# Keys of a head quad in chunks of 128, 128 and 52, with both parts of the last chunk in one operand

## What is computed

```python
Q = (query @ Wq.T).reshape(B, T_q, N_HEADS, D_HEAD)
K = (context @ Wk.T).reshape(B, T_c, N_HEADS, D_HEAD)
V = (context @ Wv.T).reshape(B, T_c, N_HEADS, D_HEAD)
scores = jnp.einsum('bqhd,bkhd->bhqk', Q, K) / scale
attn = jax.nn.softmax(scores, axis=-1)
out = jnp.einsum('bhqk,bkhd->bqhd', attn, V).reshape(B, T_q, D)
return out @ Wo.T
```

## Time and profile before

| | |
|---|---|
| median of 3 runs | 2478.12 us (2477.07 to 2478.74) |
| span of the profiled execution, first to last instruction | 2474.6 us |
| PE busy | 2404.0 us (97%), 11592 matmuls |
| DVE, ACT, POOL busy | 1171.6, 942.9, 467.3 us |

### The profile page before, as it was taken

The page is one execution under the profiler, slowest core; times in us unless marked ns, Lnnn a source line. Parts: engine busy times, 40 slices in busy tenths (PEclk is TensorE's granted clock), DMA queues, the critical chain, the costliest instruction groups (busy, mean ns, idle before and its releaser), DMA issues.

```text
span 2474.6 us, 33004 instructions
## 1 busy us (share of the span) xinstructions
PE 2404.0 (97%) x11592; PEld 1975.2 (80%) x11592; DVE 1171.6 (47%) x1978; ACT 942.9 (38%) x1505; POOL 467.3 (19%) x554
## 2 busy tenths in 40 slices
PE   8998799999999999999999999999999999999999
PEld 4877578888888887788888888888888888888887
DVE  4999688888888887532212222212212212212211
ACT  3997444445444453443233223222222323323221
POOL 3777222222222222111001001001101101101100
PEclk9999989999999999999999999999999999999999
DMA  9454701211112111400000000000000000000000
GB/s 340 174 180 161 236 1 47 66 34 68 44 34 68 39 52 68 162 1 35 34 0 34 34 17 17 34 25 9 34 34 0 34 34 0 34 34 0 34 17 17
DMA packets 83115, 141.23 MB, mean 57 GB/s; under 512 B 18022, under 2 KB 18534, under 8 KB 82662
## 3 DMA queue, kind: packets, MB, share of 16 engines
q1 hardware_dynamic: 83072, 140.68, 16.4%
HBM read 79.42 MB, written 61.24 MB: 57 GB/s over the span
## 4 chain that ended last, share of the span: by engine, by line
PE 88%; DVE 5%; DMA 3%; issue 2%; ACT 1%; DVEq 1%; SPq 0%; POOL 0%; ACTq 0%
PE ps L359 76%; PE ps L1496 5%; PE ps L1476 2%; DMA xa<-in_x 1%; DMA x_scratch<-xa 1%; PE ps L1390 1%; DVE xa L1090 1%; DVE st L986 1%; PE ps L1329 1%; PE ps L1409 1%; PE ps L1354 1%; PE ps L1308 0%; DVE ql L1015 0%; DVE xt L1015 0%; DVE es L1192 0%
## 5 line engine op out<-in xcount | busy, mean ns | idle before, releaser
L1015 DVE TENSOR_TENSOR gtl<-ps,gth 128x512 fp32r<-128x512 f32 x256 | 177.1, 692 | 1088.9 <-ACT gth L904 1088.9
L359 PE MATMUL ps<-xt,wuh 128*128 (+1 forms) x2048 | 638.2, 393 | 5.0 <-DVE xt L1015 4.9
L902 ACT ACTIVATE ps<-ps,up_b 128x512 f32<-128x512 f32 x256 | 169.5, 662 | 990.2 <-PE ps L359 990.2
L359 PEld LDWEIGHTS ps<-xt,wuh 128*128 128x128 f32 x2048 | 383.6, 188 | 93.4 <-DVE xt L1015 8.9
L359 PE MATMUL ps<-wdl,gth 128*128 128x512 f32 x1024 | 402.3, 393 | 0.0
L359 PE MATMUL ps<-wdh,gtl 128*128 128x512 f32 x1024 | 402.1, 393 | 0.0
L359 PE MATMUL ps<-wdh,gth 128*128 128x512 f32 x1024 | 402.0, 393 | 0.0
L359 PE MATMUL ps<-xt,wul 128*128 (+1 forms) x1024 | 400.6, 391 | 0.0
L607 POOL TENSOR_TENSOR rstd<-var_e,mhalf 128x4 f32<-128x4 f32 x48 | 53.2, 1109 | 1306.6 <-DVE var_e L1004 1306.6
L668 POOL TENSOR_TENSOR es<-es,rinv 128x308 f32<-128x308 f32 x256 | 171.0, 700 | 447.0 <-DVE rinv L1203 447.0
L359 PEld LDWEIGHTS ps<-wdh,gth 128*128 128x128 f32 x1024 | 192.2, 188 | 44.1
(11 more groups left out here) (186 smaller groups left out, 3765.5 us busy)
## 6 DMA issues: line engine op xcount, KB each, us to landing
x<-x_scratch SPq DMA_DIRECT2D x32, 1024.0 KB, 5.6
xa<-in_x SPq DMA_DIRECT2D x16, 1024.0 KB, 5.4
x_scratch<-xa SPq DMA_DIRECT2D x16, 1024.0 KB, 4.3
x_scratch<-x SPq DMA_DIRECT2D x16, 1024.0 KB, 4.4
out_x<-x SPq DMA_DIRECT2D x16, 1024.0 KB, 4.3
xu<-in_wexpT SPq DMA_DIRECT2D x4, 1024.0 KB, 18.5
yd<-in_wcon SPq DMA_DIRECT2D x4, 1024.0 KB, 9.3
wd_scratch<-fold SPq DMA_DIRECT2D x4, 1024.0 KB, 7.3
```

Of the source, the lines that this page charges most:

```text
L359: mm = pe.matmul(bank, a, b, start=first and i == 0, stop=last and i == n - 1)
L902: A(bank, bank, ACT.Gelu, bias=up_b[:, m:m + 1]).then_inc(act_gelu, 1)
L1015: sub = lambda o, a, b: V.tensor_tensor(o, a, b.bitcast(F32), ALU.subtract)
```

## The change

The chunks become 128, 128 and 52 keys (`KT`). Chunk 2 now holds only keys of the last head, and its high and low probabilities share one tile `pt2`: the high part in partitions 0 to 51, written by ACT, the low part in partitions 64 to 115 (`KB` = 64), written by DVE. Its values are loaded twice, at partitions 0 and 64. One matmul of `pt2` with `vh` gives high*high and low*high, and one with `vl` gives high*low, and low*low besides, which the kernel before leaves out. values(f) has 8 matmuls for 9; the value columns are 64, 128 and 128. The transposes stay 12 a tile, of 128, 128 and 66 columns. `pt2` must be zero between its parts, so POOL zeroes it once, after `fold_stored[2]` and `fold_stored[3]`, and ACT and DVE wait for `p_zero` before their first write. A value load issues 14 DMAs for 12. The buffers from `es` on move, and the tiles of the folded weights with them, so that one pair of them is loaded a step later at the start of the feed-forward.

```diff
     KC = D // P
     HPC = P // HD
     CK = HPC * L
-    KP = (CK + 2) // 3
-    CKP = 3 * KP
-    NJ = KC * 3
-    V_AT = [0, 2 * HD, 5 * HD, 9 * HD]
+    KT = CK - 2 * P
+    KB = P // 2
+    KU = KB + 2
+    CKP = 2 * P + KU
+    VW = [2 * HD, HPC * HD, HPC * HD]
+    V_AT = [0, VW[0], VW[0] + VW[1], sum(VW)]
+    assert 2 * L <= P + L and 2 * P < CK <= 2 * P + KB
     MC = HID // P
     LOS = 7
     HIS = 4
...
     assert r2.at <= yd_at
     es = [r2.put(f"es{i}", [P, KC, CKP], F32) for i in range(2)]
     free_es1 = r2.at - 4 * KC * CKP
-    vh = r2.put("vh", [KP, KC, V_AT[3]], F32R)
-    vl = r2.put("vl", [KP, KC, V_AT[3]], F32R)
+    vh = r2.put("vh", [P, KC, V_AT[3]], F32R)
+    vl = r2.put("vl", [P, KC, V_AT[3]], F32R)
     free_last = r2.at
     woh = r2.put("woh", [P, KC, D], F32R)
     wo_raw = nc.alloc_sbuf_tensor_at("wo_raw", [P, KC, D], F32, offset=r2.at)
     wol = r2.put("wol", [P, KC, D], F32R)
     assert r2.at <= wgu_at
     free_values = r2.at
-    pth = r2.put("pth", [KP, NJ, GT], F32R)
-    ptl = r2.put("ptl", [KP, NJ, GT], F32R)
+    pth = r2.put("pth", [P, 2 * KC, GT], F32R)
+    ptl = r2.put("ptl", [P, 2 * KC, GT], F32R)
+    pt2 = r2.put("pt2", [P, KC, GT], F32R)
     free_last2 = r2.at
     aoh = r2.put("aoh", [P, KC, GT], F32R)
     aol = r2.put("aol", [P, KC, GT], F32R)
...
         wq_loaded, wq_hi, wq_lo = sem("wq_loaded"), sem("wq_hi"), sem("wq_lo")
         wo_loaded, wo_hi, wo_lo = sem("wo_loaded"), sem("wo_hi"), sem("wo_lo")
         k_zero, v_zero, k_loaded, v_loaded = sem("k_zero"), sem("v_zero"), sem("k_loaded"), sem("v_loaded")
+        p_zero = sem("p_zero")
         xn2_ready = sem("xn2_ready")
         pre_pe, pre_hi, pre_lo = sem("pre_pe"), sem("pre_hi"), sem("pre_lo")
         pe_slot, act_hi, dve_slot = sem("pe_slot"), sem("act_hi"), sem("dve_slot")
...
         for h in range(HPC):
             r = 0
             while r < L:
-                c, at = divmod(h * L + r, KP)
-                n = min(L - r, KP - at)
-                pieces.append((h, r, n, c, at))
+                c, at = divmod(h * L + r, P)
+                n = min(L - r, P - at)
+                pieces += [(h, r, n, c, at)] + [(h, r, n, c, at + KB)] * (c == 2)
                 r += n
-        assert [(h, c) for h, _, _, c, _ in pieces] == [(0, 0), (1, 0), (1, 1), (2, 1), (2, 2), (3, 2)]
+        assert [(h, c) for h, _, _, c, _ in pieces] == [(0, 0), (1, 0), (1, 1), (2, 1), (3, 1), (3, 2), (3, 2)]
 
         def split3(pe, bank, parts, first=True, last=True):
 
...
                 nc.gpsimd.memset(kh[:, b].bitcast(F32), 0.0)
                 nc.gpsimd.memset(kl[:, b].bitcast(F32), 0.0).then_inc(k_zero, 1)
             pool.wait_ge(v_zero, 1)
+            for j in (2, 3):
+                pool.wait_ge(fold_stored[j], 16 * 2)
+            nc.gpsimd.memset(pt2[:, :, :].bitcast(F32), 0.0).then_inc(p_zero, 1)
 
             def norm(g, has):
                 if not has(0):
...
                     act.wait_ge(pe_slot, SLOTS * g + n + 1)
                     bank = ps[:, 4 + n % 4, :]
                     if len(out.shape) == 3:
-                        bank = bank[0:KP].rearrange("p (j n) -> p j n", j=4)
+                        bank = bank[0:out.shape[0]].rearrange("p (j n) -> p j n", j=4)
                     his.done(A(out, bank, ACT.Copy), hi_slot(n))
 
                 def hi_p(t, d):
                     if has(d):
-                        for q in range(3):
-                            hi(pth[:, 4 * q:4 * q + 4, t * P:(t + 1) * P], P_SLOT[t] + q)
+                        for q, part in ((0, pth[:, 0:KC]), (1, pth[:, KC:2 * KC]), (2, pt2[0:KT])):
+                            hi(part[:, :, t * P:(t + 1) * P], P_SLOT[t] + q)
 
                 def hi_x(c):
                     if has(1):
...
                 if isinstance(g, int) and g == 0:
                     for j in range(4):
                         act.wait_ge(fold_stored[j], 16 * 2)
+                    act.wait_ge(p_zero, 1)
                 hi_p(0, 0)
                 hi_x(2)
                 exp(2)
...
                     dve.wait_ge(act_hi, HI_SLOTS * g + hi_slot(n) + 1)
                     bank = ps[:, 4 + n % 4, :]
                     if len(out.shape) == 3:
-                        bank = bank[0:KP].rearrange("p (j n) -> p j n", j=4)
+                        bank = bank[0:out.shape[0]].rearrange("p (j n) -> p j n", j=4)
                     los.done(sub(out, bank, hi), n)
 
                 def lo_p(t, d):
                     if has(d):
-                        for q in range(3):
-                            part = lambda w: w[:, 4 * q:4 * q + 4, t * P:(t + 1) * P]
-                            lo(part(ptl), part(pth), P_SLOT[t] + q)
+                        for q, part, high in ((0, ptl[:, 0:KC], pth[:, 0:KC]), (1, ptl[:, KC:2 * KC], pth[:, KC:2 * KC]),
+                                              (2, pt2[KB:KB + KT], pt2[0:KT])):
+                            tok = slice(t * P, (t + 1) * P)
+                            lo(part[:, :, tok], high[:, :, tok], P_SLOT[t] + q)
 
                 def lo_x(c):
                     if has(1):
...
                 if isinstance(g, int) and g == 0:
                     for j in range(4):
                         dve.wait_ge(fold_stored[j], 16 * 2)
+                    dve.wait_ge(p_zero, 1)
                 lo_p(0, 0)
                 shift(2)
                 lo_x(2)
...
                     for q in range(3):
                         b = bank(P_SLOT[t] + q)
                         for j in range(4):
-                            f, c = divmod(4 * q + j, 3)
-                            mm = pe.transpose(b[0:KP, j * P:(j + 1) * P], es[t % 2][:, f, c * KP:(c + 1) * KP], ident[:, :])
+                            keys = es[t % 2][:, j, q * P:min(q * P + P, CKP)]
+                            mm = pe.transpose(b[0:keys.shape[1], j * P:(j + 1) * P], keys, ident[:, :])
                         slots.done(mm, P_SLOT[t] + q)
 
                 def turn_x(c):
...
                         pe.wait_ge(dve_slot, SLOTS * g + P_SLOT[3] + 3)
                         pe.wait_ge(v_loaded, (g + GB - 1) // GB * 16 * 2 * len(pieces))
                     b = bank(V_SLOT[f])
-                    passes = [(c, v, pt) for c in (2, 1, 0) for v, pt in ((vh, pth), (vh, ptl), (vl, pth))]
+                    passes = [(c, v, pt[:, KC * c + f, :]) for c in (1, 0) for v, pt in ((vh, pth), (vh, ptl), (vl, pth))]
+                    passes[3:3] = [(2, v, pt2[:, f, :]) for v in (vh, vl)]
                     passes.append(passes.pop(1))
                     for i, (c, v, pt) in enumerate(passes):
-                        mm = pe.matmul(b[0:(c + 2) * HD], v[:, f, V_AT[c]:V_AT[c + 1]], pt[:, 3 * f + c, :],
+                        mm = pe.matmul(b[0:VW[c]], v[:, f, V_AT[c]:V_AT[c + 1]], pt,
                                        start=(i == 0), stop=(i == len(passes) - 1))
                     slots.done(mm, V_SLOT[f])
 
```

## The result

The changed kernel takes 2486.51 us (median of five runs, 2485.06 to 2486.64); the kernel before took 2477.07 beside it (five runs, 2474.69 to 2478.74). The ratio is 1.0037, with a 95% interval of 1.0026 to 1.0048: **slower by 0.37%**. The forecast of 2482.0 is 4.5 us too low; the measured time lies on the upper end of the range, 2486.5, and the likeliest outcome, "within 0.2%", did not come.

The account below looks back on a forecast made before the run. PE was taken to set the pace, with DVE's run limiting the gain: 13.1 us start cost less 9.2 gained adds 3.9 to the 2474.6 span, 2478.5, plus 3.5 to the median: 2482.0 us; range 2476.0 to 2486.5.

Parts of the forecast that it names:

- within 0.2%: Outcome class for the whole kernel: time within 5.0 us of before, up to 2483.1 us; chance 0.57.
- The start: Start of the attention: POOL's memset waits for the fold's stores and delays scores(0) by 11.4 us.
- Rival A: Start of the attention: the wait costs nothing, giving 2468.9 us; chance 0.08.
- The clock term: First score tiles after the idle start: low TensorE clock adds 1.4 us, then 0.3 on the second tile.
- Rival B: From scores(0) to the first queries: the low clock lasts, 3.5 us more, giving 2485.5 us; chance 0.20.
- The gate at values(2): Middle bodies: values(2) waits for DVE's low part of values(0), starting only 0.07 us earlier after some 0.4 us wait.
- Rival C: Middle bodies: DVE's gate at values(2) does not bind, each gains 0.92 us, giving 2476.9 us; chance 0.10.
- I take the same 0.68: DVE's low part of `pt2`, written to other partitions: 0.68 us as before, so no added cost.
- the middle bodies: Attention loop: 13 bodies gain 0.53 us each, 6.9 us in all.
- DVE's 1.06 us of idle time: Ahead of DVE's values(3) row: this slack lets values(2) and values(3) save their 0.46 us in full.
- Moved buffers at nothing: Start of the feed-forward: one pair of folded weights loaded later, some 30 us ahead of use, costed at nothing.
- 3.5 us above the span: Whole kernel: the median was put this far above the profiled span, turning 2478.5 into 2482.0 us.

Follow-up runs that it names:

- e1: Changed kernel with POOL's wait for the two stores and the memset of `pt2` moved behind the factors of group 1's norm; 2473.79 us, ratio 0.9990.
- e5: Kernel before, nine matmuls kept, with only the wait for the two stores and a 2048-element memset ahead of group 1's norm; 2489.1 us, ratio 1.0047.
- e3: Kernel before with 64 unused bytes a partition ahead of the output projection's weights; 2454.64 us, ratio 0.9914.
- e11: Repeat of e3, the kernel before with 64 unused bytes; 2454.19 us, ratio 0.9915.
- e4: Changed kernel with DVE writing the last chunk's low part to partitions 0 to 51 (output not the reference's); 2483.69 us in one run.
- e6: e1 with DVE's low part of values(0) put between the maximum and the subtraction of shift(1); 2474.44 us, ratio 0.9992.
- e9: e7 with ACT copying values(1) ahead of exp(1) and DVE making its low part ahead of sums(1); 2436.31 us, ratio 0.9841.
- e2: Changed kernel with 640 unused bytes a partition ahead of the output projection's weights; 2484.0 us, ratio 1.0030.
- e12: Kernel before, nine matmuls, with 64 unused bytes and the order of e9 on ACT and DVE; 2450.04 us, ratio 0.9907.
- e8: Kernel before with 192 unused bytes a partition ahead of the output projection's weights; 2478.84 us in one run.
- e7: e6 with 64 unused bytes ahead of the value tiles and 640 ahead of the output projection's weights; 2448.45 us, ratio 0.9886.

## Why the forecast came out too low, and why the range still held

**The start was right.** Each step came within 0.7 us: memset at 289.15 (forecast 288.5) for 1.80 us (1.9), factors at 290.92 (290.4), scores(0) at 297.02 (296.5). The 0.5 us at its end were there when the memset began, so the work behind it was costed right. (The working rounds up twice: 288.4 + 1.9 is 290.3, and 291.7 + 2.8 is 294.5.) The base of this sum is less firm than its steps: before's 285.11 is late among the starts without the wait, 281.1 to 285.7. Rival A, that it costs nothing, is out by e1 and e5.

**The clock term was a guess of the right kind, and not settled.** scores(0) did run at the low level, at 3.25 us. But the second tile ran at the high one, and up to the first values after was 0.8 us faster than before. Windows from scores(0) to the first values, before and after, in columns as in the earlier trace rows:

```profile
285.00:340.00 55.00, 36.88 (x185) 32.54 (x186) 40.28 (x54) 21.93 (x32) 11.99 (x19) 0.81 0.28 78
```

```profile
297.00:351.00 54.00, 37.09 (x185) 32.18 (x186) 39.06 (x51) 20.32 (x30) 11.91 (x18) 0.82 0.12 37
```

The mean granted clock is 0.81 and 0.82. The two profiles of one kernel, e3 and e11, have 0.74 with 54.69 us and 0.87 with 52.16; e5, the kernel before with the wait, has 0.74 with 56.95. A term of 1.7 can't be checked with one profile each in a stretch that differs by 2.5 us between two profiles of the same kernel. Rival B (the low level lasts, 2485.5) is nearest to the measured time, but for another reason: its mechanism is not in the trace of after.

**The gate at values(2) was the right mechanism, mis-sized.** Rival C fell: PE waits there in every body, 0.05 us behind `aol`, as forecast. The step that failed is "I take the same 0.68" for the low part written to other partitions. The text had said that each 0.1 us there would be 1.3 us in the end; the rows put it at 0.22 us, and e4 at 0.26, with the body at 43.97 for 44.23. The duration is 0.68, just as taken; what I missed is that it is the distance to the neighbours that fills a run, 0.71 + 0.71 for 0.60 + 0.60. In sum, the middle bodies gave 13 x 0.22 = 2.9 us for the 6.9 forecast, and the others 1.4 for 2.3. The part of this in the miss is 4.9 us, of which the low part on other partitions is 13 x 0.26 = 3.4.

A second thing was incomplete: I counted DVE's 1.06 us of idle time as cover for all that stands behind values(2). e6 shows that the next gates are close behind the first one: with it open, the body stayed at 44.23. Rival C, with 0.92 a body, therefore needed more than an early `aol`; e9's order gives 0.87.

**Moved buffers at nothing: wrong, and not in the sum at all.** I had costed a transfer of the feed-forward's weights and never their new addresses. That is +3.5 us by the sections; e2 takes back 2.5 by the medians. The Trainium skill ("TensorE: Matmul & The Clock Gate", section "Step-by-step: what each phase is for") says that loading the next weights does not steal read bandwidth from the running matmul; no run here tests that, since whether it is the loads, the streamed operand or the accesses of other engines that collide is not told apart. What the runs show is that 64 bytes moved the time by 0.9%.

**The sum.** Misses by the sections: +0.5 start, -2.5 clock, +4.9 gain, +3.5 addresses: 6.4 us above the 3.9 forecast, which gives the 10.2 us of the spans to 0.1. By medians it is 9.4, and the runs of one kernel spread over 1.0 to 6.6 us (e11, e12), so no part is known better than to about 2 us from medians alone.

**Why the time still lies in the range: partly luck.** From span to span the forecast was 6.3 us too low (2478.5 for 2484.8), and from median to median only 4.5. The prediction had put the median 3.5 us above the span, as in the profile of before; in after it is 1.7 above. That 1.8 us, and the 2.5 of the clock, went against the 8.4 us of the gain and the addresses. The upper end of the range had been set for a low clock that lasts (rival B), and not for either of these two.

## What to carry to other kernels

Removing work from the engine that sets the pace brings only what the next chain lets through, and that chain may have several gates close behind each other; read the distance between starts in its run, not the durations, and look what each in-order queue holds behind an instruction that waits for a third engine. A wait for a late transfer holds everything behind it in its queue, here for 12 to 13 us of 2477, and moved behind two short instructions it was free. When a change moves buffers, compare the distances of neighbouring matmuls in stretches that the change doesn't touch: 1.4% of a body, as between before and e3, can hide behind a PE that is busy 99.6% both times.

## What was not expected of the hardware

**Matmul spacing by address.** With shapes and granted clock alike, the feed-forward's matmuls of 512 columns start 226.7 ns apart when all folded weights and their partners lie at the same position modulo 2048 bytes (1472), and 229 to 234 ns apart for weights at 1408, 768 and 1600. An equal position is not the rule for every matmul: the output projection's `woh`, `wol`, `aoh` and `aol` share one position in every kernel (1408 before, 768 after, 1472 in e3, 1600 in e8), and their mean distances are 229.6, 230.8, 230.2 and 230.5 ns. Only four positions were tried in the feed-forward, all against partners at 1472, so neither the period nor the rule is settled. Open too is why the distance in values(3) is 0.2295 us in after and 0.233 in e7, where `vh` moved by 64 bytes and the probabilities by 704; in e2, where `vh` stays and the probabilities move by 640, it is 0.232.

**A VectorE result on other partitions.** A subtraction of 52 partitions with 512 elements, written to other partitions than it reads, keeps its 0.68 us and loses 0.11 us of overlap on each side (e4: 0.60 between starts, after: 0.71).

**The same stretch at the start of the attention**, from scores(0) to the first values, took 54.7 us at a mean granted clock of 0.74 and 52.2 at 0.87 in two profiles of one kernel (e3, e11). The clock alone does not order the times: before has 54.6 us at 0.81.
